# Regrouping the MLP products between the transform slots of a spectral block on TensorE

## Chip, cores and metric

The kernel runs on one core of a Trainium2 chip. The metric is the device time of one execution in microseconds (us). Three runs of the kernel before gave 3795.04, 3796.38 and 3802.16 us, so its median is 3796.38 us.

## What is computed

Four layers follow each other on `x` of shape (4, 64, 128, 128): a box convolution, four spectral blocks (`L1_conv`, which is what the change touches), and two more box convolutions. One spectral block is:

```python
def _block(x, ln1w, ln1b, ln2w, ln2b, w1, w2, b1, b2, mw1, mb1, mw2, mb2):
    residual = x
    xn = _ln(transpose(x, (0, 2, 3, 1)), ln1w, ln1b)
    xf = rfft2(xn, axes=(1, 2), norm='ortho')
    o1 = relu(complex product of xf with w1 + b1)      # 64 x 64 channels
    o2 = complex product of o1 with w2 + b2
    o2 = o2 where |re| > 0.01 or |im| > 0.01, else 0
    x = residual + irfft2(o2)
    h = gelu(_ln(x, ln2w, ln2b) @ mw1 + mb1)           # 64 -> 256
    return x + (h @ mw2 + mb2)                         # 256 -> 64
for i in range(4): x = _block(x, ...)
```

All arithmetic is in float32.

## The kernel before

`afno_layers` works through 16 runs (4 images by 4 layers), one image and layer at a time. All of an image's `x` lies in SBUF. The work is a hand-written software pipeline. A period `n` belongs to run `n` and has 16 steps `q` = 0 to 15, and each step has four slots `s` = 0 to 3. In every step the MLP of run `n` advances by one block of 8 image rows. In the slots the transforms run: the last four inverse products of run `n`, and then forward transform, spectrum, backward transform and first four inverse products of run `n + 1`. Since periods begin at n = -2, the first transform (n = -1) has no MLP beside it, and the last period (n = 15) has no forward transform. Fifteen periods, n = 0 to 14, have both.

Which unit of the transform stands in which slot is set by these lines, where a slot's number is `4 * q + s`:

```python
REST_SLOTS = (3, 7, 17, 18)
FORWARD_SLOT, SPECTRUM_SLOT, BACKWARD_SLOT = 19, 23, 44
NEXT_SLOTS = (48, 49, 51, 53)
```

- `inverse`: a product into two PSUM banks; VectorE (three additions), ScalarE (one copy, `odd`) and GpSimd finish it. Products 4 to 7 of a run stand in slots 3, 7, 17 and 18, so products 6 and 7 are in step 4, slots 1 and 2.
- `forward`: slots 19 to 22, four units of four 128x128 matmuls each (L1629). VectorE and ScalarE take turns copying the result into `g`, four small operations for one unit. The wait before unit 2 is for `s_x` of the last inverse product: `if i == 2 and n: pe.wait_ge(s_x, INVERSES * n)`.
- `spectrum`: slots 23 to 41 hold `t` = 0 to 18. On TensorE each holds three products of three successive chunks: mix2 (L1640, chunk t-2, reads `o1`), mix1 (L1649, chunk t-1, reads `xf`), and fh (L1658, chunk t). ScalarE turns mix1's result into `o1` (L1473) and fh's into `xf` (L1480). VectorE turns mix2's result into `o2` (L1336). Chunk 0 is a quarter as wide as the others. Before fh of chunk 0, TensorE waits for all copies of the forward transform, and for a `memset` of VectorE (L1329) that itself waits for ScalarE's copies.
- `backward`: slots 44 to 47, after GpSimd's masked products of every chunk (L1259).
- `inverse` 0 to 3 of the next run: slots 48, 49, 51, 53.

The MLP of a step is, on TensorE: `mlp_up(Q, 0)` and `mlp_up(Q, 1)` (L1683, 64 rows of the array to a matmul), `mlp_down(Q - 1)` (L1694, 64 columns to a matmul), `turn_back(Q - 2)` (L1709) and `turn(Q + 1)` (L1703), both transposes on the full array. ScalarE does gelu (L1507) after each `mlp_up`, `operand` (L1513) after `turn` and `mlp_delta` (L1520) after `mlp_down`. VectorE's `residual` (L1364) adds the result to `x` after `turn_back`, and the next `mlp_down` waits for it. VectorE's `sum_up` and `root` and ScalarE's `square` (layer-norm statistics), in slots of their own, and ScalarE's `fill_stage` stay where they are.

Each engine walks the periods and steps in its own loop, and its instruction order is the order of that code.

Of the kernel before, what the change touches and what calls it, by code (L numbers as in the profile page):

```python
# [1009 lines left out]
def afno_layers(nc, const, w, src, dst):  # L1010


    with ExitStack() as ctx:
# [118 lines left out]
        with nc.Block() as block:  # L1132
# [146 lines left out]
            def _(dve):  # L1279
# [120 lines left out]
                for n, q in periods():  # L1400
                    Q, r = BLOCKS * n + q, SETS * n + q // 4
                    parts(n, q, 0, inverse, forward, spectrum, backward)
                    if 0 <= Q - 2 < BLOCKS * RUNS:
                        residual(Q - 2)
                    for s in range(1, 4):
                        parts(n, q, s, inverse, forward, spectrum, backward)
                        if s == (3 if q in (5, 12) else 1):
                            for strip in strips_at(n, q):
                                sum_up(*strip)
                        if FIRST_ROOT <= r < END_ROOT:  # L1410
                            if q in (1, 13) and s == 1:
                                root(r, range(ROOT_STEPS))
                            if (q, s) in ((5, 3), (9, 2)):
                                root(r, range(ROOT_STEPS // 2))
                            if (q, s) in ((6, 1), (9, 3)):
                                root(r, range(ROOT_STEPS // 2, ROOT_STEPS))

            @block.scalar
            def _(act):
# [135 lines left out]
                for n, q in periods():  # L1555
# [6 lines left out]
                    parts(n, q, 0, inverse, forward, spectrum, backward)  # L1562
                    if 0 <= Q + 1 < BLOCKS * RUNS:
                        operand(Q + 1)
                    parts(n, q, 0, other, other, magnitude, other)
# [10 lines left out]
                    parts(n, q, 2, inverse, forward, spectrum, backward)  # L1576
                    if 0 <= Q - 1 < BLOCKS * RUNS:
                        mlp_delta(Q - 1)
                    parts(n, q, 2, other, other, magnitude, other)
# [11 lines left out]
            def _(pe):  # L1591
# [120 lines left out]
                for n, q in periods():  # L1712
# [4 lines left out]
                    parts(n, q, 0, inverse, forward, spectrum, backward)  # L1717
                    if 0 <= Q - 2 < BLOCKS * RUNS:
                        turn_back(Q - 2)
                    if 0 <= Q + 1 < BLOCKS * RUNS:  # L1720
                        turn(Q + 1)
                    parts(n, q, 1, inverse, forward, spectrum, backward)
                    if mlp:
                        mlp_up(Q, 1)
                    parts(n, q, 2, inverse, forward, spectrum, backward)
                    if 0 <= Q - 1 < BLOCKS * RUNS:
                        mlp_down(Q - 1)
                    parts(n, q, 3, inverse, forward, spectrum, backward)
# [57 lines left out]
```

## Time and profile before

| | us |
|---|---|
| median of three runs | 3796.38 |
| the profiled execution | 3798.83 |
| its span | 3796.9 |
| TensorE (PE) matmul busy in the span | 3299.8 |
| VectorE (DVE) busy | 2437.3 |
| ScalarE (ACT) busy | 2377.3 |
| GpSimd (POOL) busy | 1713.5 |

In the profile, PE is TensorE's matmuls and PEld its weight loads. A float32 matmul is recorded in passes, so "x8" stands for four matmuls. The end of a matmul is modelled and lies inside the next one, so the cost of a product is read from its start to the start of the next. The spectral blocks take the stretch from about 377 to 3310 us of the span.

### The profile page before, as it was taken

How to read it: one execution, taken by the hardware profiler on the slowest of the kernel's cores; microseconds unless marked ns; L12 is line 12 of the kernel's file. 1: busy time of each engine (PE TensorE's matmuls, PEld its weight loads, DVE VectorE, ACT ScalarE, POOL GpSimd, SP SyncE). 2: the span in 40 equal slices, each digit the busy share in tenths (PEclk: the TensorE clock that was granted, in tenths of full speed). 3: DMA queues.
4: the chain of work that ended last, by engine and by line, in shares of the span. 5: the costliest groups of instructions: out<-in, count | busy, mean ns of one | idle time of the engine just before them, and what ended most of it. 6: DMA issues, size and time to landing. Idle time of an engine off the chain costs nothing. (4 is left out here: it accounts for less than half of the span.)

```text
span 3796.9 us, 54132 instructions
## 1 busy us (share of the span) xinstructions
PE 3299.8 (87%) x18664; PEld 2009.6 (53%) x18664; DVE 2437.3 (64%) x4175; ACT 2377.3 (63%) x3944; POOL 1713.5 (45%) x1397
## 2 busy tenths in 40 slices
PE   2951879999999999898999999999999999777479
PEld 0641746555565646464646464646555565255247
DVE  1843675767676667676766667575757655369567
ACT  0852566667676757676766666666657665547358
POOL 2404445445555554545445454545545533234232
PEclk9985989999999999999999999999999999989779
DMA  9871111111111111213121111111101111263798
GB/s 226 251 249 60 45 50 40 56 39 62 45 45 50 45 45 45 111 45 133 45 84 45 50 40 51 40 50 45 62 29 62 45 45 51 58 263 117 186 261 245
DMA packets 235117, 334.15 MB, mean 88 GB/s; under 512 B 38624, under 2 KB 163680, under 8 KB 228720
## 3 DMA queue, kind: packets, MB, share of 16 engines
q1 hardware_dynamic: 198112, 298.44, 23.2%
q10 hardware_dynamic: 28784, 18.44, 2.1%
q0 software_dynamic: 7968, 13.99, 1.5%
q8 instruction: 147, 2.41, 0.3%
q14 instruction: 106, 0.87, 0.1%
HBM read 183.99 MB, written 146.80 MB: 87 GB/s over the span
## 5 line engine op out<-in xcount | busy, mean ns | idle before, releaser
L1507 ACT ACTIVATE a_hidden<-a_wide,a_up_b 128x1024 f32<-128x1024 f32 x512 | 569.8, 1113 | 136.4 <-PE a_wide L1683 135.0
L1683 PE MATMUL a_wide<-a_yc,a_up_fold 64*128 64x512 f32 x2048 | 583.5, 645 | 52.8 <-ACT a_hidden L1507 48.5
L1694 PE MATMUL a_result<-a_hidden,a_down 128*64 128x512 f32 x2048 | 516.1, 625 | 67.4 <-DVE a_x L1364 66.0
L1259 POOL TENSOR_TENSOR a_y<-a_o,a_mag 128x256 f32<-128x256 f32 (+1 forms) x512 | 365.4, 739 | 385.6 <-DVE a_mag L1353 385.6
L1217 POOL TENSOR_TENSOR a_y<-a_x,a_stat 128x512 f32<-128x512 f32 x256 | 267.9, 1047 | 483.8 <-DVEq L1398 463.6
L1336 DVE TENSOR_TENSOR a_o<-a_bank,a_mix_b 128x512 f32<-128x512 f32 (+1 forms) x272 | 181.6, 668 | 278.4 <-PE a_bank L1640 274.3
L1520 ACT ACTIVATE a_delta<-a_result,a_down_b 128x512 f32<-128x512 f32 x256 | 176.3, 689 | 263.6 <-PE a_result L1694 263.5
L1658 PEld LDWEIGHTS a_bank<-a_dft_h,a_g 128*128 128x128 f32 x2080 | 272.4, 191 | 129.0 <-issue 129.0
L1640 PEld LDWEIGHTS a_bank<-a_mix,a_o 128*128 128x128 f32 x2080 | 252.8, 191 | 150.8 <-issue 132.9
L1205 POOL TENSOR_TENSOR a_x<-a_x,a_odd 128x512 f32<-128x512 f32 (+1 forms) x128 | 161.2, 1259 | 367.9 <-DVE a_x L1306 298.2
L1364 DVE TENSOR_TENSOR a_x<-a_result,a_x 128x512 f32<-128x512 f32 x256 | 176.1, 688 | 225.5 <-PE a_result L1709 223.3
L1694 PEld LDWEIGHTS a_result<-a_hidden,a_down 128*64 128x64 f32 x2048 | 131.3, 139 | 355.5 <-issue 321.3
L1640 PE MATMUL a_bank<-a_mix,a_o 128*128 128x128 f32 x2080 | 298.3, 285 | 5.9 <-DVE a_o L1336 4.1
L1683 PEld LDWEIGHTS a_wide<-a_yc,a_up_fold 64*128 64x128 f32 x2048 | 159.5, 187 | 265.8 <-issue 235.9
L1383 DVE TENSOR_REDUCE a_stat<-a_sq 128x16 f32<-128x1024 f32 x240 | 290.9, 1212 | 11.1 <-ACT a_sq L1541 9.4
L1629 PE MATMUL a_bank<-a_dft_w,a_y 128*128 128x128 f32 x2048 | 245.8, 279 | 57.9 <-POOL a_y L1242 57.6
L1629 PEld LDWEIGHTS a_bank<-a_dft_w,a_y 128*128 128x128 f32 x2048 | 235.6, 193 | 93.1 <-POOL a_y L1242 57.7
L1658 PE MATMUL a_bank<-a_dft_h,a_g 128*128 128x128 f32 x2080 | 277.3, 275 | 1.8 <-DVE a_g L1329 1.8
L1381 DVE TENSOR_REDUCE a_stat<-a_x 128x16 f32<-128x1024 f32 x224 | 271.5, 1212 | 1.9 <-issue 0.2
L1649 PE MATMUL a_bank<-a_xf,a_mix_fold 128*128 128x512 f32 (+1 forms) x544 | 270.0, 578 | 0.8 <-ACT a_xf L1480 0.8
L1673 PEld LDWEIGHTS a_bank<-a_dft_hi,a_y 128*128 128x128 f32 x2048 | 235.7, 193 | 53.7 <-POOL a_y L1259 30.1
L1673 PE MATMUL a_bank<-a_dft_hi,a_y 128*128 128x128 f32 x2048 | 245.8, 279 | 17.5 <-POOL a_y L1259 17.5
(191 smaller groups left out, 6370.1 us busy)
## 6 DMA issues: line engine op xcount, KB each, us to landing
a_x<-rows SPq DMA_DIRECT2D x112, 512.0 KB, 4.5
rows<-a_x SPq DMA_DIRECT2D x112, 512.0 KB, 2.9
box_x<-in_x SPq DMA_DIRECT2D x64, 256.0 KB, 4.3
turned<-box_o SPq DMA_DIRECT2D x64, 256.0 KB, 3.6
a_y<-turned SPq DMA_DIRECT2D x16, 1024.0 KB, 11.0
box_x<-rows SPq DMA_DIRECT2D x16, 1024.0 KB, 24.1
turned<-box_work SPq DMA_DIRECT2D x64, 256.0 KB, 2.0
box_x<-turned SPq DMA_DIRECT2D x64, 256.0 KB, 3.8
```

The lines of the kernel that those rows point to most:

```text
L1217: G.tensor_tensor(rows(y2[:, i % 2]), x[:, row:row + HB], r[:, :, None].broadcast_to([P, HB, C]), ALU.mult).then_inc(s_y2, 1)
L1259: ins = G.tensor_tensor(y[n % 2][:, :, to].rearrange("p c k -> p k c"), o2[:, j % 3, lo:4, r], mask[:, lo:4], ALU.mult)
L1381: V.tensor_reduce(stat[:, 0, r % SETS, kind - 1, u * SH:(u + 1) * SH], strip, AX.X, ALU.add)
L1383: V.tensor_reduce(stat[:, 1, r % SETS, kind - 1, u * SH:(u + 1) * SH], squares_of(r, kind, u), AX.X, ALU.add).then_inc(s_sq_read, 1)
L1507: A(hidden[:, i % 2, j], wide[:], ACT.Gelu, bias=up_b2[:, l, j:j + 1]).then_inc(s_hid, 1)
L1629: mm = M(bank[i % 4][:, c * P:(c + 1) * P], y[n % 2][:, 4 * i + c, :], dft_w[:], start=True, stop=True)
L1640: mm = M(bank[3][:, k * P:(k + 1) * P], o1[:, k * P:(k + 1) * P], mix2[:, l], start=True, stop=True)
L1649: M(bank[2][:, 0:cols], mix1_fold[:, l], xf[:, 0:cols], start=True, stop=True).then_inc(s_mix1, 1)
L1658: mm = M(bank[0][:, k * P:(k + 1) * P], g[:, first_kw(t) + k].rearrange("p r c -> p (r c)"), dft_h[:], start=True, stop=True)
L1673: mm = M(bank[i % 4][:, c * P:(c + 1) * P], y[n % 2][:, 4 * i + c, :], dft_hi[:], start=True, stop=True)
L1683: mm = M(wide[:, half * BANK:(half + 1) * BANK], up_fold[cs, l, j * P:(j + 1) * P], yc[cs, i % 2], start=True, stop=True)
L1694: mm = M(result[half * C:(half + 1) * C, :], down[:, l, j, :], hidden[:, i % 2, j, half * BANK:(half + 1) * BANK], start=j == 0, stop=j == ...
```

## The change

Three of the engines' loops are reordered inside a step. Nothing is added or removed. On TensorE the step was up(0), slot 0, turn_back, turn, slot 1, up(1), slot 2, down, slot 3. It becomes up(0), turn_back, turn, slot 0, slot 1, up(1), down, slot 2, slot 3. ScalarE's and VectorE's steps follow.

```diff
 # VectorE
                 for n, q in periods():
                     Q, r = BLOCKS * n + q, SETS * n + q // 4
-                    parts(n, q, 0, inverse, forward, spectrum, backward)
                     if 0 <= Q - 2 < BLOCKS * RUNS:
                         residual(Q - 2)
+                    parts(n, q, 0, inverse, forward, spectrum, backward)
 # ScalarE
-                    parts(n, q, 0, inverse, forward, spectrum, backward)
                     if 0 <= Q + 1 < BLOCKS * RUNS:
                         operand(Q + 1)
+                    parts(n, q, 0, inverse, forward, spectrum, backward)
                     parts(n, q, 0, other, other, magnitude, other)
...
-                    parts(n, q, 2, inverse, forward, spectrum, backward)
                     if 0 <= Q - 1 < BLOCKS * RUNS:
                         mlp_delta(Q - 1)
+                    parts(n, q, 2, inverse, forward, spectrum, backward)
                     parts(n, q, 2, other, other, magnitude, other)
 # TensorE
                     if mlp:
                         mlp_up(Q, 0)
-                    parts(n, q, 0, inverse, forward, spectrum, backward)
                     if 0 <= Q - 2 < BLOCKS * RUNS:
                         turn_back(Q - 2)
                     if 0 <= Q + 1 < BLOCKS * RUNS:
                         turn(Q + 1)
+                    parts(n, q, 0, inverse, forward, spectrum, backward)
                     parts(n, q, 1, inverse, forward, spectrum, backward)
                     if mlp:
                         mlp_up(Q, 1)
-                    parts(n, q, 2, inverse, forward, spectrum, backward)
                     if 0 <= Q - 1 < BLOCKS * RUNS:
                         mlp_down(Q - 1)
+                    parts(n, q, 2, inverse, forward, spectrum, backward)
                     parts(n, q, 3, inverse, forward, spectrum, backward)
```

TensorE, step 5 of a period, from its second `mlp_up`: the last forward units (L1629), fh of chunk 0 (the first L1658) and what follows. Before:

```order
L1683 MATMUL a_wide<-a_yc,a_up_fold 128x512 x2
L1629 MATMUL a_bank0<-a_dft_w,a_y0 128x128 x4
L1629 MATMUL a_bank1<-a_dft_w,a_y0 128x128 x4
L1629 MATMUL a_bank2<-a_dft_w,a_y0 128x128 x4
L1629 MATMUL a_bank3<-a_dft_w,a_y0 128x128 x4
L1694 MATMUL a_result<-a_hidden,a_down 64x512 x4
L1658 MATMUL a_bank0<-a_dft_h,a_g 128x128
L1683 MATMUL a_wide<-a_yc,a_up_fold 128x512 x2
```

The same place in the changed kernel:

```order
L1683 MATMUL a_wide<-a_yc,a_up_fold 128x512 x2
L1694 MATMUL a_result<-a_hidden,a_down 64x512 x4
L1629 MATMUL a_bank0<-a_dft_w,a_y0 128x128 x4
L1629 MATMUL a_bank1<-a_dft_w,a_y0 128x128 x4
L1629 MATMUL a_bank2<-a_dft_w,a_y0 128x128 x4
L1629 MATMUL a_bank3<-a_dft_w,a_y0 128x128 x4
L1658 MATMUL a_bank0<-a_dft_h,a_g 128x128
L1683 MATMUL a_wide<-a_yc,a_up_fold 128x512 x2
```

`mlp_down` (L1694) stood between the last forward unit and fh of chunk 0. It now stands ahead of the forward units, and fh follows the last of them directly.

TensorE, step 4, from inverse product 6 on (L1611 and L1615 are one inverse product). Before:

```order
L1611 MATMUL a_bank0<-a_g,a_idft_e 128x512
L1615 MATMUL a_bank1<-a_g,a_idft_o 128x512
L1683 MATMUL a_wide<-a_yc,a_up_fold 128x512 x2
L1611 MATMUL a_bank2<-a_g,a_idft_e 128x512
L1615 MATMUL a_bank3<-a_g,a_idft_o 128x512
L1694 MATMUL a_result<-a_hidden,a_down 64x512 x4
L1629 MATMUL a_bank0<-a_dft_w,a_y0 128x128 x4
L1629 MATMUL a_bank1<-a_dft_w,a_y0 128x128 x4
```

The same place in the changed kernel:

```order
L1611 MATMUL a_bank0<-a_g,a_idft_e 128x512
L1615 MATMUL a_bank1<-a_g,a_idft_o 128x512
L1683 MATMUL a_wide<-a_yc,a_up_fold 128x512 x2
L1694 MATMUL a_result<-a_hidden,a_down 64x512 x4
L1611 MATMUL a_bank2<-a_g,a_idft_e 128x512
L1615 MATMUL a_bank3<-a_g,a_idft_o 128x512
L1629 MATMUL a_bank0<-a_dft_w,a_y0 128x128 x4
L1629 MATMUL a_bank1<-a_dft_w,a_y0 128x128 x4
```

`mlp_down` stood between inverse product 7 and the forward transform. It now stands ahead of product 7.

TensorE, step 6, from mix2 of the first chunk (the fourth row is the second `mlp_up`). Changed kernel:

```order
L1640 MATMUL a_bank3<-a_mix2,a_o1 128x128
L1649 MATMUL a_bank2<-a_xf,a_mix1_fold 128x512
L1658 MATMUL a_bank0<-a_dft_h,a_g 128x128 x4
L1683 MATMUL a_wide<-a_yc,a_up_fold 128x512 x2
L1694 MATMUL a_result<-a_hidden,a_down 64x512 x4
L1640 MATMUL a_bank3<-a_mix2,a_o1 128x128 x4
L1649 MATMUL a_bank2<-a_xf,a_mix1_fold 128x512
L1658 MATMUL a_bank0<-a_dft_h,a_g 128x128 x4
L1640 MATMUL a_bank3<-a_mix2,a_o1 128x128 x4
L1649 MATMUL a_bank2<-a_xf,a_mix1_fold 128x512
L1658 MATMUL a_bank0<-a_dft_h,a_g 128x128 x4
```

Before, `mlp_down` stood between the second and the third group of L1640, L1649 and L1658 shown here. Now those two groups touch, and `mlp_up` and `mlp_down` touch.

## Rows read from the trace of the kernel before

**Rows 1.** The page's first part: busy us, share, instructions.

```profile
PE 3299.8 (87%) x18664; PEld 2009.6 (53%) x18664; DVE 2437.3 (64%) x4175; ACT 2377.3 (63%) x3944; POOL 1713.5 (45%) x1397
```

**Rows 2.** Waits of PE, 380:3350: total us, times, longest.

```profile
PE a_result L1694 <- DVE a_x L1364: 66.0, 41, 2.5
```

**Rows 3.** Timeline of PE in a spectrum step: start, us, instructions.

```profile
1506.78 1.06 PE L1640 MATMUL a_bank<-a_mix,a_o 128*128 128x128 f32 x8
1507.68 1.02 PE L1649 MATMUL a_bank<-a_xf,a_mix_fold 128*128 128x512 f32 x2
1508.54 1.05 PE L1658 MATMUL a_bank<-a_dft_h,a_g 128*128 128x128 f32 x8
1509.52 1.13 PE L1683 MATMUL a_wide<-a_yc,a_up_fold 64*128 64x512 f32 x4
1510.58 1.16 PE L1640 MATMUL a_bank<-a_mix,a_o 128*128 128x128 f32 x8
1511.58 1.02 PE L1649 MATMUL a_bank<-a_xf,a_mix_fold 128*128 128x512 f32 x2
...
1513.42 1.94 PE L1694 MATMUL a_result<-a_hidden,a_down 128*64 128x512 f32 x8
1515.29 1.16 PE L1640 MATMUL a_bank<-a_mix,a_o 128*128 128x128 f32 x8
```

**Rows 4.** Timeline of PE, transform without MLP (n = -1), idle in brackets.

```profile
396.80 0.46 PE L1658 MATMUL a_bank<-a_dft_h,a_g 128*128 128x128 f32 x2 [1.84 <-DVE a_g L1329]
...
397.95 1.06 PE L1658 MATMUL a_bank<-a_dft_h,a_g 128*128 128x128 f32 x8
398.85 0.39 PE L1640 MATMUL a_bank<-a_mix,a_o 128*128 128x128 f32 x2
399.70 1.13 PE L1649 MATMUL a_bank<-a_xf,a_mix_fold 128*128 128x512 f32 x2 [0.46 <-ACT a_xf L1480]
...
403.61 1.05 PE L1658 MATMUL a_bank<-a_dft_h,a_g 128*128 128x128 f32 x8
404.55 1.16 PE L1640 MATMUL a_bank<-a_mix,a_o 128*128 128x128 f32 x8
405.55 1.02 PE L1649 MATMUL a_bank<-a_xf,a_mix_fold 128*128 128x512 f32 x2
```

**Rows 5.** Timeline of PE, end of the spectrum to the backward transform.

```profile
1521.98 1.16 PE L1640 MATMUL a_bank<-a_mix,a_o 128*128 128x128 f32 x8
1523.07 1.13 PE L1683 MATMUL a_wide<-a_yc,a_up_fold 64*128 64x512 f32 x4
1524.13 1.94 PE L1694 MATMUL a_result<-a_hidden,a_down 128*64 128x512 f32 x8
1526.00 1.13 PE L1683 MATMUL a_wide<-a_yc,a_up_fold 64*128 64x512 f32 x4
1527.96 3.84 PE L1673 MATMUL a_bank<-a_dft_hi,a_y 128*128 128x128 f32 x32 [0.83 <-POOL a_y L1259]
```

**Rows 6.** Timelines of PE, ACT and DVE at the end of the forward transform.

```profile
1635.51 1.94 PE L1694 MATMUL a_result<-a_hidden,a_down 128*64 128x512 f32 x8
1637.42 0.46 PE L1658 MATMUL a_bank<-a_dft_h,a_g 128*128 128x128 f32 x2
...
1635.62 1.34 ACT L1456 ACTIVATE a_g<-a_bank 64x252 f32<-64x252 f32 x4 [0.45 <-PE a_bank L1629]
...
1637.11 0.17 DVE L1329 MEMSET a_g<- 1x128 f32 x1 [0.83 <-ACT a_g L1456]
```

**Rows 7.** Timelines of PE and DVE at inverse product 6.

```profile
1611.85 1.02 PE L1615 MATMUL a_bank<-a_g,a_idft_o 128*128 128x512 f32 x2
...
1614.33 0.69 DVE L1310 TENSOR_TENSOR a_x<-a_bank,a_x 128x512 f32<-128x512 f32 x1
```

**Rows 8.** Timelines at the next run's inverse product 2, and two steps on.

```profile
1557.37 0.69 DVE L1305 TENSOR_TENSOR a_x<-a_bank,a_x 128x512 f32<-128x512 f32 x1 [2.92 <-PE a_bank L1615]
...
1573.12 3.49 PE L1694 MATMUL a_result<-a_hidden,a_down 128*64 128x512 f32 x8 [2.35 <-DVE a_x L1364]
```

## The prediction, made before the changed kernel was run

> **What bounds the kernel now.** The page's first part puts TensorE at 3299.8 us of matmul in a span of 3796.9 us, with VectorE and ScalarE at about two thirds [rows 1]. The waits of PE over the spectral blocks say how little is left: the largest cause, `mlp_down` waiting for VectorE's `residual`, is 66.0 us in 41 waits [rows 2]. So in these blocks TensorE is the bound, its products run back to back, and a change pays what it saves in TensorE's pitch (start of one product to start of the next) and costs what it uncovers as waits. I then read one spectrum step in PE's timeline for the pitch [rows 3], and as a model of touching slots the one transform that has no MLP beside it, n = -1 [rows 4].
>
> **What it saves.** Full-array products, `mlp_up` (64 rows) and `mlp_down` (64 columns) use the array in three shapes. Four 128x128 matmuls take 0.90 us between full-array neighbours: fh 397.95 to 398.85 [rows 4], mix2 after a transpose 1506.78 to 1507.68 [rows 3]. Before an `mlp_up` fh takes 0.98 us (1508.54 to 1509.52), and mix2 behind it takes 1.00 (1510.58 to 1511.58) [rows 3]. So leaving the full shape costs 0.08 and coming back 0.10. `mlp_up` itself costs 1.06 whether a full-array product follows (1509.52 to 1510.58) [rows 3] or `mlp_down` (1523.07 to 1524.13), and `mlp_down` costs 1.87 before either (1513.42 to 1515.29 [rows 3], 1524.13 to 1526.00 [rows 5]). The change removes a return and a departure only where slot 2 is not empty, because elsewhere up(1) and down touch already. Those are steps 4 to 9 and 11, seven of a period. That is 7 x 0.18 = 1.26 us a period, and over the 15 periods that have both MLP and transforms 19 us. The exit after up(0) stays, in front of `turn_back` instead of slot 0, and I count it as nothing.
>
> The Trainium skill, "TensorEngine Tiling (Array Packing)", section Tiling Modes, says that changing the tiling mode drains TensorE. It gives no price. The rows agree, with 0.08 to 0.10 us for each edge, except that up to down shows none beyond what up always costs.
>
> **What it uncovers.** Four places, each once a period except the third.
>
> First, fh of chunk 0. It waits for the last forward unit's four ScalarE copies and VectorE's `memset` after them. Now `mlp_down` covers this: it starts at 1635.51 when the forward units are through, the copies start at 1635.62, the `memset` at 1637.11, fh at 1637.42 [rows 6]. That is 1.91 us, of which down's 1.87 is work. After the change down stands ahead of the forward units and nothing is left between. Bounds: 1.84, which is what the transform without MLP waits at this very place [rows 4], and 1.91. I take 1.9.
>
> Second, mix1 of chunk 1. It needs `xf`, made from the fh just before it, with only the small mix2 of chunk 0 between. Until now the two transposes lay there too. Without MLP mix1 starts 0.85 us after that mix2 [rows 4], which is one matmul of four, a quarter of 0.90, so 0.22. That leaves 0.63, and 0.10 more because a weight load that follows a wait is not hidden (below). I take 0.73, with the row's idle of 0.46 as the lower bound.
>
> Third, the steady spectrum pairs. In touching slots mix2 follows the mix1 of its own chunk with only one fh between, and ScalarE needs slightly longer for `o1`: fh to mix2 takes 0.94 instead of 0.90, and mix2 1.00 instead of 0.90 [rows 4]. That is 0.14 for each second slot. The pairs are slots 26-27 to 38-39, seven of them, hence 1.0 us a period. Lower bound 0.04 x 7 = 0.3. Pair 24-25 is the second place. In the last pair, 40-41, mix2 follows mix1 of its own chunk with nothing between, and waits about 0.9 for `o1`. But the backward transform waits 0.83 today for GpSimd's end of a chain that starts from this same mix2, 5.98 us before it (1521.98 to 1527.96) [rows 5]. The transposes move from before that mix2 to behind up(0), so they leave one wait and fill the other. Net nothing; if the first wait were covered after all, this would give 0.83 x 15 = 12 us.
>
> Fourth, forward unit 2 waits for `x` of inverse product 7. At product 6 the last addition of VectorE starts at 1614.33 and takes 0.69, so it ends 3.17 us after the second matmul starts at 1611.85 [rows 7]. Until now down (1.87) and two units lay over this. Now it is the rest of the product, 0.86 for a 512-wide matmul [rows 3], and two units of 0.90, together 2.66. That uncovers 0.51, and 0.10 for the weight load: 0.6, between 0.4 and 0.7.
>
> ScalarE's `operand` and `mlp_delta` move ahead of slots 0 and 2. Their inputs (`turn`, `mlp_down`) are now finished when those slots' products start, so no `o1` or `xf` is queued behind a waiting one. VectorE's `residual` is likewise earlier in its queue, and its input too. I cost these at nothing. The cover is the slots' own products ahead of the first result; if it fails, it costs up to one such operation's 0.7 us in a step.
>
> Sum of a period: 1.9 + 0.73 + 1.0 + 0.6 = 4.23 uncovered, less 1.26 saved, is 2.97. Times 15 that is +45 us. The profiled execution took 3798.8 us, so it would take 3844. The median of the runs shown is 2.4 us lower, which gives **3841 us**, 1.2% slower.
>
> **Rivals.**
>
> *The clock falls as well.* After one of its waits TensorE runs a `mlp_down` in 3.49 us, which is the 1.2 GHz level, instead of 1.94 at 2.4 GHz [rows 8, 3]. A new idle of 1.9 us before chunk 0, followed by short work, could bring one more such drop a period: 1.55 x 15 = 23 us, so 3864. Against it: the same idle without MLP is followed by fh at 1.06, full speed [rows 4]. [...] Chance 0.10.
>
> *Faster: the lost time is given back.* TensorE waits for VectorE's backlog in steps 13 and 14, most of the 66.0 us [rows 2]. If that backlog ran on a clock of its own, lateness from earlier in the period would shorten those waits, and only the savings would be left: 3796 - 19 = 3777. It turns into a gain once 2.97 of the 4.23 us a period are recovered. Against it: VectorE's chain there starts after 2.92 us of its own idle, released by TensorE's inverse product [rows 8], so it shifts with TensorE. Chance 0.04.
>
> *No difference.* Only the first place opens, and pairs and inverse product stay covered: 15 x (1.9 - 1.26) = 10 us, and with the last pair's 12 us recovered about nothing, 3794 to 3804. The rows of the transform without MLP speak against it. Chance 0.06.
>
> *Forecast.* Chance 0.80. With all lower bounds (1.84 + 0.46 + 0.3 + 0.4 = 3.0) it is +26 us, 3822; with the upper ones (1.91 + 0.73 + 1.3 with the last pair + 0.7, less 1.26) it is +51, 3847. An end effect or the clock now and then widens this upwards.
>
> **How the numbers follow.** About 0.2%, 8 us, is what a measurement can tell from no change. Slower takes the forecast and the clock, 0.90; same 0.06; faster 0.04. The range for 8 in 10 is 3815 to 3866: it reaches the clock rival above, leaves out the two below.
>
> **What would show it.** Right: PE's waits gain a group at L1658 released by DVE L1329, 15 times some 1.9 us; one at L1649 from ACT, 15 x 0.5; one at L1629 from DVE L1310, 15 x 0.5; and a touching mix2 starts 0.94 after fh. The backward wait (L1673 on GpSimd) shrinks, and one at L1640 from ACT of about 0.9 appears. The waits of steps 13 and 14 stay. Wrong: waits of L1694 that shrink by microseconds a period, or an L1658 that starts at once.

## The result, and the profile of the changed kernel

The changed kernel takes 3858.97 us (median of 4 runs, 3851.67 to 3862.81), the kernel before 3799.2 us in the runs beside it (3795.04 to 3802.16). The ratio is 1.0156, with a 95% interval of 1.0136 to 1.0175. So it is 1.6% slower, 60 us by the medians and 53 us by the profiled executions (3851.67 against 3798.83). The forecast was +45 us. One execution of the kernel of experiment 8 took 9350.06 us, its eleven others 3790 to 3804 us; it is left out of that kernel's ratio.

The first part of the page of the changed kernel, which answers to [rows 1] (busy us, share, instructions):

```profile
PE 3316.7 (86%) x18664; PEld 2016.0 (52%) x18664; DVE 2433.5 (63%) x4175; ACT 2367.9 (62%) x3944; POOL 1708.9 (44%) x1397
```

The same instructions run, and TensorE's busy time has grown by 17 us only. The rest of the 53 is waiting. The waits of PE over 380 to 3400 us (line and releaser, total us, times, longest):

```profile
PE a_result L1694 <- DVE a_x L1364: 67.7, 42, 2.7
...
PE a_bank L1658 <- DVE a_g L1329: 29.3, 16, 1.8
...
PE a_bank L1640 <- ACT a_o L1473: 15.3, 21, 0.9
...
PE a_bank L1673 <- POOL a_y L1259: 8.4, 15, 4.9
...
PE a_bank L1649 <- ACT a_xf L1480: 6.3, 17, 0.5
PE a_bank L1629 <- DVE a_x L1310: 4.9, 15, 0.3
```

Each group that was forecast is there. The first one, `mlp_down` behind VectorE's `residual`, stood at 66.0 [rows 2]: nothing is given back there. One wait of each transform group belongs to n = -1, as in [rows 4].

To place the time I cut each of the 15 periods at four starts on TensorE: the first forward unit (L1629), fh of chunk 0 (L1658), the first backward product (L1673) and the 64-wide inverse product (L1613). One such period in PE's timeline of the changed kernel (start us, us, instruction, idle before it):

```profile
2382.18 1.95 PE L1629 MATMUL a_bank<-a_dft_w,a_y 128*128 128x128 f32 x16
2384.45 0.71 PE L1629 MATMUL a_bank<-a_dft_w,a_y 128*128 128x128 f32 x4 [0.32 <-DVE a_x L1310]
...
2404.26 0.46 PE L1658 MATMUL a_bank<-a_dft_h,a_g 128*128 128x128 f32 x2 [1.83 <-DVE a_g L1329]
...
2478.92 1.27 PE L1673 MATMUL a_bank<-a_dft_hi,a_y 128*128 128x128 f32 x9 [0.24 <-POOL a_y L1259]
...
2499.38 0.33 PE L1613 MATMUL a_bank<-a_g,a_idft_e 128*128 128x64 f32 x2
...
2566.02 1.95 PE L1629 MATMUL a_bank<-a_dft_w,a_y 128*128 128x128 f32 x16
```

The lengths are 22.08, 74.66, 20.46 and 66.64 us. In most periods a stretch repeats within 0.02 us unless the clock falls in it, which adds about 1.6 us, as in the last of these (65.00 without). Three periods in the middle of the execution differ, in the kernel before too. The table gives, for the kernels of this study but those of experiments 6 and 10, the length that a period without a fallen clock has. The transposes of one step lie on the other side of two of the cuts when the first group is moved (about 0.9 us goes from the last stretch to the second), so across kernels the sum is what compares.

| us | forward | spectrum | backward | inverse | period |
|---|---|---|---|---|---|
| before | 19.77 | 72.57 | 20.70 | 65.97 | 179.01 |
| changed | 22.08 | 74.67 | 20.46 | 65.00 | 182.21 |
| first group alone | 19.72 | 74.43 | 20.61 | 65.09 | 179.85 |
| second group alone | 22.12 | 72.87 | 20.50 | 65.87 | 181.36 |
| TensorE's order alone | 22.08 | 74.25 | 20.42 | 65.06 | 181.81 |
| down back in step 5 | 20.20 | 74.68 | 20.46 | 65.00 | 180.34 |
| down back in steps 4, 5 | 19.73 | 74.69 | 20.46 | 65.09 | 179.97 |
| roots a slot earlier | 22.07 | 74.26 | 20.41 | 64.99 | 181.73 |
| all four undone | 19.73 | 73.58 | 20.41 | 65.09 | 178.81 |
| edges only | 19.77 | 72.36 | 20.50 | 65.95 | 178.58 |

A period is 3.20 us longer, where 2.97 were forecast. That is 48 us over 15 periods. The other part is the clock. From fh of chunk 0 to the backward transform five of the 15 periods take 76.27 to 76.31 us instead of 74.67, and none did before: 5 x 1.61 = 8 us. From the first cut to the last the changed kernel takes 61.5 us more (2863.3 against 2801.7). Of the remaining 5 us about 4 lie in two periods, those that start at 1635.98 and 1826.01 us. They are longer in the kernel before too, but the change opens three more waits in each: mix2 waits 0.52 and 0.44 us for ScalarE's `o1`, and a backward product waits 1.06 us for ScalarE. ScalarE's, then PE's timeline there:

```profile
1736.69 2.00 ACT L1552 ACTIVATE a_stage<-a_y 128x1024 f32<-128x1024 f32 x1 [2.90 <-POOL a_y L1229]
...
1739.72 1.49 PE L1673 MATMUL a_bank<-a_dft_hi,a_y 128*128 128x128 f32 x11 [1.06 <-ACT a_g L1499]
```

L1552 is `fill_stage`, 2.00 us long. Of the 15 periods only these two hold it beside the spectrum and the backward transform. That it causes the three waits is read from the rows; no run moves it.

In the profiled execution the parts ahead of the first cut and behind the last gave 4.8 and 3.9 us back, hence 53 there and 60 by the medians.

Here is the clock. PE's timeline behind fh of chunk 0, in a period where it falls, then in one where it does not:

```profile
2218.76 0.46 PE L1658 MATMUL a_bank<-a_dft_h,a_g 128*128 128x128 f32 x2 [1.83 <-DVE a_g L1329]
2219.14 1.60 PE L1683 MATMUL a_wide<-a_yc,a_up_fold 64*128 64x512 f32 x4
2220.68 1.11 PE L1709 MATMUL a_result<-a_ident,a_delta 128*128 128x128 f32 x4
2221.58 1.06 PE L1703 MATMUL a_turned<-a_ident,a_y 128*128 128x128 f32 x4
...
2404.65 1.13 PE L1683 MATMUL a_wide<-a_yc,a_up_fold 64*128 64x512 f32 x4
2405.71 0.66 PE L1709 MATMUL a_result<-a_ident,a_delta 128*128 128x128 f32 x4
2406.20 0.60 PE L1703 MATMUL a_turned<-a_ident,a_y 128*128 128x128 f32 x4
...
2406.86 1.06 PE L1658 MATMUL a_bank<-a_dft_h,a_g 128*128 128x128 f32 x8
2407.76 0.48 PE L1640 MATMUL a_bank<-a_mix,a_o 128*128 128x128 f32 x2
2408.61 1.12 PE L1649 MATMUL a_bank<-a_xf,a_mix_fold 128*128 128x512 f32 x2 [0.37 <-ACT a_xf L1480]
2409.57 1.05 PE L1658 MATMUL a_bank<-a_dft_h,a_g 128*128 128x128 f32 x8
...
2415.34 1.05 PE L1658 MATMUL a_bank<-a_dft_h,a_g 128*128 128x128 f32 x8
2416.28 1.16 PE L1640 MATMUL a_bank<-a_mix,a_o 128*128 128x128 f32 x8
2417.27 1.02 PE L1649 MATMUL a_bank<-a_xf,a_mix_fold 128*128 128x512 f32 x2
```

The windows of the same two places (us, busy us and instructions of PE, PEld, DVE, ACT and POOL, then the granted clock as a share of 2.4 GHz, DMA share, GB/s):

```profile
2220.20:2222.60 2.40, 2.40 (x11) 1.93 (x10) 2.19 (x8) 1.11 (x1) 0.00 (x0) 0.50 0.00 0
2405.70:2408.10 2.40, 2.40 (x22) 2.32 (x20) 2.19 (x8) 2.01 (x4) 0.00 (x0) 1.00 0.00 0
```

Half of 2.4 GHz is granted in the one, the whole of it in the other. The idle ahead of both is the same 1.83 us. The second timeline also shows the second place of the forecast: mix1 of chunk 1 (2408.61) waits 0.37 us for ScalarE's `xf` and starts 0.85 us after mix2 of chunk 0, and 0.96 us pass until the next fh. Ahead of the change these two pitches were 0.22 and 0.86, so this place costs 0.73. The last three rows are a touching pair: mix2 starts 0.94 us after fh, and mix1 0.99 after mix2, the pitches of [rows 4].

A saving that the forecast counted as nothing is in these rows too. Behind `mlp_up` stands now `turn_back`, which takes 0.49 us to the next start (2405.71 to 2406.20). In the kernel before it stood behind a full-array product:

```profile
1505.91 0.60 PE L1709 MATMUL a_result<-a_ident,a_delta 128*128 128x128 f32 x4
1506.35 0.60 PE L1703 MATMUL a_turned<-a_ident,a_y 128*128 128x128 f32 x4
```

There it took 0.44, but the mix2 behind `mlp_up` took 1.00, where behind the transposes it takes 0.90 [rows 3]. So the return to the full array is 0.05 us cheaper in each of the seven steps (5 to 10 and 12) that have a product in slot 0 and no wait that takes it up, about 0.35 us a period.

One number stands where the forecast expected nothing. At the end of the spectrum, PE's and then DVE's timeline:

```profile
2472.51 1.16 PE L1640 MATMUL a_bank<-a_mix,a_o 128*128 128x128 f32 x8 [0.78 <-ACT a_o L1473]
...
2470.39 0.23 DVE L1005 SCALAR_TENSOR_TENSOR a_stat<-a_stat 128x64 f32<-128x64 f32 x1
2470.76 0.69 DVE L1364 TENSOR_TENSOR a_x<-a_result,a_x 128x512 f32<-128x512 f32 x1
2471.37 0.68 DVE L1336 TENSOR_TENSOR a_o<-a_bank,a_mix_b 128x512 f32<-128x512 f32 x1
```

The wait of the last mix2 for `o1` (0.78 us) is the one forecast. But from that mix2 to the backward product 6.41 us pass (2472.51 to 2478.92), where it was 5.98 [rows 5]. VectorE doesn't wait for TensorE here: behind the second half of `root` (it ends with L1005) comes `residual` (L1364), and only then `o2` (L1336), 1.14 us before the mix2 of the chunk after it. The experiments take this place apart.

### The profile page after: what moved, and what is told of

Read it like the earlier page. It is cut to its first block and busy times, and to the rows that moved or that the text cites. A ratio compares the mean times of both kernels' runs of the same rounds, so it can differ in the third digit from the quotient of the medians.

```text
span 3849.8 us, 54132 instructions
## 1 busy us (share of the span) xinstructions
PE 3316.7 (86%) x18664; PEld 2016.0 (52%) x18664; DVE 2433.5 (63%) x4175; ACT 2367.9 (62%) x3944; POOL 1708.9 (44%) x1397
## 5 line engine op out<-in xcount | busy, mean ns | idle before, releaser
L1694 PE MATMUL a_result<-a_hidden,a_down 128*64 128x512 f32 x2048 | 513.9, 623 | 69.1 <-DVE a_x L1364 67.7
L1336 DVE TENSOR_TENSOR a_o<-a_bank,a_mix_b 128x512 f32<-128x512 f32 (+1 forms) x272 | 181.3, 667 | 309.8 <-PE a_bank L1640 308.4
L1364 DVE TENSOR_TENSOR a_x<-a_result,a_x 128x512 f32<-128x512 f32 x256 | 176.4, 689 | 288.3 <-PE a_result L1709 283.9
L1658 PEld LDWEIGHTS a_bank<-a_dft_h,a_g 128*128 128x128 f32 x2080 | 273.3, 192 | 147.2 <-issue 147.2
L1694 PEld LDWEIGHTS a_result<-a_hidden,a_down 128*64 128x64 f32 x2048 | 131.0, 138 | 413.6 <-issue 404.7
L1640 PE MATMUL a_bank<-a_mix,a_o 128*128 128x128 f32 x2080 | 297.9, 285 | 18.6 <-ACT a_o L1473 15.3
L1473 ACT ACTIVATE a_o<-a_bank,a_mix_b 128x512 f32<-128x512 f32 (+2 forms) x272 | 181.2, 666 | 201.2 <-PE a_bank L1649 201.2
L1658 PE MATMUL a_bank<-a_dft_h,a_g 128*128 128x128 f32 x2080 | 277.9, 276 | 29.3 <-DVE a_g L1329 29.3
L1640 PEld LDWEIGHTS a_bank<-a_mix,a_o 128*128 128x128 f32 x2080 | 253.0, 191 | 90.8 <-issue 52.4
L1629 PE MATMUL a_bank<-a_dft_w,a_y 128*128 128x128 f32 x2048 | 243.8, 278 | 62.7 <-POOL a_y L1242 57.6
L1629 PEld LDWEIGHTS a_bank<-a_dft_w,a_y 128*128 128x128 f32 x2048 | 236.4, 193 | 85.2 <-POOL a_y L1242 57.7
L1649 PE MATMUL a_bank<-a_xf,a_mix_fold 128*128 128x512 f32 (+1 forms) x544 | 271.5, 581 | 6.3 <-ACT a_xf L1480 6.3
L1673 PE MATMUL a_bank<-a_dft_hi,a_y 128*128 128x128 f32 x2048 | 239.6, 278 | 10.6 <-POOL a_y L1259 8.4
```

What stands on the lines that cost most here:

```text
L1629: mm = M(bank[i % 4][:, c * P:(c + 1) * P], y[n % 2][:, 4 * i + c, :], dft_w[:], start=True, stop=True)
L1640: mm = M(bank[3][:, k * P:(k + 1) * P], o1[:, k * P:(k + 1) * P], mix2[:, l], start=True, stop=True)
L1649: M(bank[2][:, 0:cols], mix1_fold[:, l], xf[:, 0:cols], start=True, stop=True).then_inc(s_mix1, 1)
L1658: mm = M(bank[0][:, k * P:(k + 1) * P], g[:, first_kw(t) + k].rearrange("p r c -> p (r c)"), dft_h[:], start=True, stop=True)
L1673: mm = M(bank[i % 4][:, c * P:(c + 1) * P], y[n % 2][:, 4 * i + c, :], dft_hi[:], start=True, stop=True)
L1694: mm = M(result[half * C:(half + 1) * C, :], down[:, l, j, :], hidden[:, i % 2, j, half * BANK:(half + 1) * BANK], start=j == 0, stop=j == ...
```

## The experiments

Two theories stood after the result. **Lost cover**: the change opens waits at a few places of TensorE's chain of spectrum products, each of a fixed size, and the two groups add up. The rival: **order on the other engines**, by which moving `operand`, `residual` and `mlp_delta` ahead of slots delays the copies that the slots' products need, and so makes the loss. A third, the **clock**, could hold most of it. Below, diffs against the kernel before are headed so; the others are against the changed kernel. Each kernel was timed 4 to 12 times beside the kernel before; stretches, waits and falls of the clock come from one profiled execution of each. In the text "q" is a step of the period.

### 1. The first group alone

Against the kernel before: of the change, only `turn_back` and `turn` on TensorE, `operand` on ScalarE and `residual` on VectorE move ahead of slot 0.

```diff
                         mlp_up(Q, 0)
-                    parts(n, q, 0, inverse, forward, spectrum, backward)
                     if 0 <= Q - 2 < BLOCKS * RUNS:
                         turn_back(Q - 2)
                     if 0 <= Q + 1 < BLOCKS * RUNS:
                         turn(Q + 1)
+                    parts(n, q, 0, inverse, forward, spectrum, backward)
```

> Only the first group: turn_back and turn stand behind up(0), slots 0 and 1 touch; slot 2 stays between up(1) and down, on all engines. Theory of uncovered waits: nothing is lost ahead of fh of chunk 0 or at forward unit 2 (down still covers both), and no array-shape edge is saved. Uncovered are mix1 of chunk 1 (0.73 us a period), three steady pairs (3 x 0.14) and, as the trace of the changed kernel showed, 0.4 us more in the chain from the last mix2 to the backward transform; the exit after up(0) gives some 0.04 a step back. Together 1.1 to 1.5 us a period, +16 to +23 us against the kernel before. Rival (the loss lies at the fh of chunk 0 alone): within 3 us of before.

3814.78 against 3798.62 us, ratio 1.0046 (1.0029 to 1.0063); a period is 0.84 us longer. Its waits of PE:

```profile
PE a_bank L1640 <- ACT a_o L1473: 15.4, 21, 0.9
...
PE a_bank L1649 <- ACT a_xf L1480: 6.1, 17, 0.4
PE a_bank L1673 <- POOL a_y L1259: 4.9, 1, 4.9
```

So this group holds mix1 of chunk 1 and the last pair. The wait of the backward product is down to the one of n = -1: here the last pair's wait does take its place, as forecast. The extra 0.4 us at the end of the spectrum, which my expectation put into this group, isn't here: the backward transform starts 6.00 us after the last mix2, although `residual` stands ahead of `o2` here too. That is why the period is 0.84 us longer and not 1.1 to 1.5: 0.73, and three steady pairs at 0.15, less 0.35 for the cheaper returns, make 0.83.

### 2. The second group alone

Against the kernel before: only `mlp_down` and `mlp_delta` move ahead of slot 2.

```diff
                         mlp_up(Q, 1)
-                    parts(n, q, 2, inverse, forward, spectrum, backward)
                     if 0 <= Q - 1 < BLOCKS * RUNS:
                         mlp_down(Q - 1)
+                    parts(n, q, 2, inverse, forward, spectrum, backward)
```

> Only the second group: down stands behind up(1), slots 2 and 3 touch; slot 0 stays ahead of turn_back, on all engines. Theory of uncovered waits: 1.9 (fh of chunk 0) + 0.6 (forward unit 2) + 4 pairs x 0.14, less 7 x 0.18 of saved edges = 1.8 us a period, +27 us, and up to +35 with the drops of TensorE's clock that follow the wait at fh of chunk 0. The backward transform's wait on GpSimd stays at about 0.8 us in each of 15 periods. Rival (the pairs of slots are what costs, wherever they lie): about half of the changed kernel's loss, with a pair as dear as one of the first group's.

3833.72 against 3798.62 us, ratio 1.0096 (1.0081 to 1.0112); a period is 2.35 us longer. Together the two groups make 0.84 + 2.35 = 3.19 us a period, and the whole change 3.20. They add up, and the second holds the larger part. Its waits of PE:

```profile
PE a_bank L1673 <- POOL a_y L1259: 24.4, 16, 4.9
```

The waits at fh of chunk 0 and at forward unit 2 are as in the changed kernel. The backward product's wait, which I expected to stay at 0.8 us, is longer than the 0.83 of [rows 5]: (24.4 - 4.9) / 15 = 1.30 us. DVE's, then PE's timeline at the end of the spectrum:

```profile
2459.47 0.23 DVE L1005 SCALAR_TENSOR_TENSOR a_stat<-a_stat 128x64 f32<-128x64 f32 x1
2459.91 0.69 DVE L1336 TENSOR_TENSOR a_o<-a_bank,a_mix_b 128x512 f32<-128x512 f32 x1 [0.21 <-DVE a_stat L1005]
...
2460.75 1.16 PE L1640 MATMUL a_bank<-a_mix,a_o 128*128 128x128 f32 x8
...
2467.19 1.05 PE L1673 MATMUL a_bank<-a_dft_hi,a_y 128*128 128x128 f32 x7 [1.30 <-POOL a_y L1259]
```

From the last mix2 to the backward product 6.44 us pass, so the late `o2` is in this group. `residual` doesn't stand ahead of it here; `root` alone does. What makes `root` late is that slots 2 and 3 of step 9, behind which its halves stand, now touch; in experiment 9 they touch as well, with `root` a slot earlier, and the backward transform is not late. With that the sum of my theory closes: its 1.8 and this 0.46 us make 2.3, against 2.35 measured.

### 3. TensorE's order alone

TensorE as in the changed kernel, ScalarE's and VectorE's calls where they stood before (`mlp_delta` moves back likewise).

```diff
+                    parts(n, q, 0, inverse, forward, spectrum, backward)
                     if 0 <= Q - 2 < BLOCKS * RUNS:
                         residual(Q - 2)
-                    parts(n, q, 0, inverse, forward, spectrum, backward)
...
+                    parts(n, q, 0, inverse, forward, spectrum, backward)
                     if 0 <= Q + 1 < BLOCKS * RUNS:
                         operand(Q + 1)
-                    parts(n, q, 0, inverse, forward, spectrum, backward)
```

> TensorE in the order of the changed kernel, ScalarE and VectorE in the order of before (operand behind slot 0, mlp_delta behind slot 2, residual behind slot 0). Theory: those moves are worth nothing in themselves, so the time is that of the changed kernel within 5 us, with the same waits at fh of chunk 0, mix1 of chunk 1 and forward unit 2. Rival (operand and delta ahead of the slots delay o1 and xf): 10 us or more faster than the changed kernel, with a touching mix2 that starts 0.90 instead of 0.94 us after fh.

3843.91 against 3798.62 us, ratio 1.0121 (1.0101 to 1.0142); a period of 181.81 us. So TensorE's order alone makes 2.80 of the 3.20 us, and the rival falls for the bulk. The time is 13 us below the changed kernel by the ratios, where I expected at most 5; the two intervals overlap slightly. The other 0.40 is real, and lies in the spectrum stretch alone (74.25 against 74.67). DVE's, then PE's timeline at the end of the spectrum:

```profile
2288.37 0.69 DVE L1336 TENSOR_TENSOR a_o<-a_bank,a_mix_b 128x512 f32<-128x512 f32 x1 [0.28 <-PE a_bank L1640]
...
2289.64 0.68 DVE L1364 TENSOR_TENSOR a_x<-a_result,a_x 128x512 f32<-128x512 f32 x1
...
2289.97 1.16 PE L1640 MATMUL a_bank<-a_mix,a_o 128*128 128x128 f32 x8 [0.78 <-ACT a_o L1473]
...
2295.97 1.23 PE L1673 MATMUL a_bank<-a_dft_hi,a_y 128*128 128x128 f32 x9
```

With `residual` behind `o2`, VectorE waits for TensorE (0.28) instead of being late, `o2` starts 1.60 us ahead of the mix2 instead of 1.14, and the backward product starts 6.00 us behind it with no wait. The last pair's 0.78 is unchanged. This run puts three calls back at once, so that it is the place of `residual` is read from these rows. TensorE's touching mix2 products keep their pitch of 0.94 and 1.00 us, so those don't come from ScalarE's or VectorE's order.

### 4. `mlp_down` back behind slot 2 in step 5

```diff
-                    if 0 <= Q - 1 < BLOCKS * RUNS:
+                    if 0 <= Q - 1 < BLOCKS * RUNS and not q == 5:
                         mlp_down(Q - 1)
                     parts(n, q, 2, inverse, forward, spectrum, backward)
+                    if 0 <= Q - 1 < BLOCKS * RUNS and q == 5:
+                        mlp_down(Q - 1)
```

`mlp_delta` on ScalarE is treated alike.

> The changed kernel, but in step 5 of every period mlp_down (TensorE) and mlp_delta (ScalarE) stand behind slot 2 again, between the last forward units and fh of chunk 0. Theory of uncovered waits: fh of chunk 0 waits 0.0 instead of 1.8 us, one return edge and one departure edge come back (0.18), so 1.7 us a period and 26 us less than the changed kernel, and the slow-clock stretches right behind fh of chunk 0 go as well (another 8 us): 26 to 34 us faster than the changed kernel, +25 to +33 against before. Rival (that wait only shifts to the next one): under 10 us faster than the changed kernel.

3817.03 against 3798.62 us, ratio 1.005 (1.0037 to 1.0064). The forward stretch falls from 22.08 to 20.20 us: fh of chunk 0 costs 1.88. The waits of PE for `memset` are gone apart from the one of n = -1, and the clock falls behind fh of chunk 0 in none of the 15 periods. So one product, left where it was, gives back 40 us of the 60 by the ratios (1.0156 to 1.005). My expectation was 26 to 34; the stretches and the falls of the clock account for 28 + 8 = 36. The 1.88 is net: the departure edge of `mlp_down` in step 5, 0.10 us, has come back with it, so the wait itself costs about 1.98.

### 5. The roots a slot earlier

The halves of VectorE's `root` in step 9 stand behind slots 1 and 2 instead of 2 and 3, so that the second is through before the last pair.

```diff
-                            if (q, s) in ((5, 3), (9, 2)):
+                            if (q, s) in ((5, 3), (9, 1)):
                                 root(r, range(ROOT_STEPS // 2))
-                            if (q, s) in ((6, 1), (9, 3)):
+                            if (q, s) in ((6, 1), (9, 2)):
                                 root(r, range(ROOT_STEPS // 2, ROOT_STEPS))
```

> The changed kernel with VectorE's two halves of root in step 9 one slot earlier (behind slots 1 and 2 instead of 2 and 3). In the changed kernel those halves stand behind two slots that now touch, VectorE comes late to the next o2, and the backward transform starts 6.4 us after the last mix2 instead of 6.0. Theory: that 0.4 us is VectorE's root, so it goes: backward starts 6.0 us after the last mix2 and the wait on GpSimd is 0, 6 us less than the changed kernel. Rival (it is ScalarE's mlp_delta or the place of residual): no difference, the distance stays at 6.4.

3840.13 against 3796.85 us, ratio 1.0125 (1.011 to 1.0139). The spectrum stretch is 74.26 us, and the backward product's wait is that of n = -1 alone:

```profile
PE a_bank L1673 <- POOL a_y L1259: 4.6, 1, 4.6
```

This is the same 0.41 us as in experiment 3, with `residual` left ahead of slot 0. In TensorE's changed order either of the two, `root` or `residual`, taken from in front of `o2` is enough: the queue of both is what is late. In the order of experiment 2 `root` alone was. By the ratios this kernel is 12 us faster than the changed one, where I expected 6. The 0.41 us make 6, and the clock falls behind fh of chunk 0 in three periods instead of five, which makes another 3.

### 6. The gap filled

Ahead of fh of chunk 0 TensorE runs eight more 128x128 matmuls of the identity into the `turned` bank. Nobody reads them, and they compute nothing of the reference.

```diff
                         if t == 0:
+                            if n:
+                                pe.wait_ge(s_yc, BLOCKS * (n - 1) + 5 + 2)
+                                for c in range(8):
+                                    M(turned[:, c % 4 * P:(c % 4 + 1) * P], ident[:], ident[:], start=True, stop=True)
                             pe.wait_ge(s_g_dve, GROUPS // 2 * (n + 1))
```

> The changed kernel with eight extra 128x128 matmuls on the identity matrix, written to the free bank of the transposes, in front of TensorE's wait at fh of chunk 0 (1.8 us of work that nobody reads). Theory: the wait itself stays, now as work; what goes are the stretches at the 1.2 GHz level that follow it in some periods (fh of chunk 0 to the backward transform takes 76.3 us there instead of 74.7). So all periods take 74.7 or less, and the whole is 0 to 8 us faster than the changed kernel, never slower by more than 2. Rival (the drops are not due to that idle): as many stretches of 76.3 as before.

3846.98 against 3796.85 us, ratio 1.013 (1.0115 to 1.0144). PE's timeline, in which L1655 is the added line:

```profile
2220.68 1.95 PE L1655 MATMUL a_turned<-a_ident 128*128 128x128 f32 x16
2222.67 0.46 PE L1662 MATMUL a_bank<-a_dft_h,a_g 128*128 128x128 f32 x2
2223.06 1.13 PE L1687 MATMUL a_wide<-a_yc,a_up_fold 64*128 64x512 f32 x4
```

The work fills the idle and fh starts no later. The forward stretch is 22.08 us as in the changed kernel, in all but two periods (22.21 and 22.37), so the 1.88 us are not a matter of the clock. The clock falls behind it in 0 of 15 periods instead of 5, which is what these falls cost: 8 us. The same count in the other profiles: 5 of 15 in experiment 2, 7 in experiment 3 and 3 in experiment 5, which all have the idle, and none in experiments 1, 4 and 7 to 10 and in the kernel before, where `mlp_down` covers it. By the ratios it is 10 us faster than the changed kernel, but the intervals (1.0115 to 1.0144, 1.0136 to 1.0175) overlap.

### 7. `mlp_down` back in steps 4 and 5

As experiment 4, with `q in (4, 5)` in place of `q == 5`.

> The kernel of e4 with mlp_down and mlp_delta behind slot 2 in step 4 as well, so that down again lies between inverse product 7 and the forward transform. Theory: forward unit 2 no longer waits for x (0.6 us a period at most; the trace of e4 puts the stage from the first forward unit to fh of chunk 0 0.43 us above before), and step 4 loses its two saved edges (0.18). So that stage returns to 19.8 us, and the kernel is 4 to 6 us faster than e4, +13 to +17 against before. Rival: the wait moves to the next forward unit and the stage stays at 20.2.

3815.61 against 3797.18 us, ratio 1.0052 (1.0039 to 1.0065), no different from experiment 4 by the medians, where I expected 4 to 6 us less. The stretches resolve what the median does not: the forward one falls by another 0.47 us (19.73), and 0.09 comes back in the inverse one, where an edge of array shapes returns. So forward unit 2 costs 0.38 us a period net, 6 us in all. The return edge of `mlp_down`, 0.10 us, lies inside the forward stretch and has come back as well, so the wait itself costs 0.57.

### 8. All four places undone

The kernel of experiment 7 with the roots a slot earlier, and in step 6 slot 0 back ahead of `turn_back` and `turn`, `operand` and `residual`. On TensorE, against experiment 7:

```diff
+                    if q == 6:
+                        parts(n, q, 0, inverse, forward, spectrum, backward)
                     if 0 <= Q - 2 < BLOCKS * RUNS:
                         turn_back(Q - 2)
                     if 0 <= Q + 1 < BLOCKS * RUNS:
                         turn(Q + 1)
-                    parts(n, q, 0, inverse, forward, spectrum, backward)
+                    if not q == 6:
+                        parts(n, q, 0, inverse, forward, spectrum, backward)
```

> The kernel of e9, with root in step 9 a slot earlier and, in step 6 only, slot 0 ahead of turn_back and turn again, so that mix1 of chunk 1 is covered. What is left of the change is grouping in steps 6 to 9 and 11 and touching slots 0 and 1 in steps 7 to 9. Theory: the account is complete, so undoing its four items takes a no-drop period from 3.2 us above before to between 0.3 below and 0.1 above, and the kernel is within 5 us of before. Rival (something else in the change costs, not in the account): 8 us or more above before, although none of the four waits is there.

3798.51 against 3797.18 us, ratio 1.0003 (0.9994 to 1.0012). The period falls from 179.97 to 178.81, by 1.16 us. Of these 0.41 are the roots (experiment 5), so mix1 of chunk 1 is worth about 0.75. The changed order of all other steps is now no loss, a period 0.20 us shorter than before, although the last pair still waits for `o1`:

```profile
PE a_bank L1648 <- ACT a_o L1476: 16.2, 22, 0.9
```

(L1648 and L1476 are L1640 and L1473 moved by the added lines.)

### 9. Edges only

Against the kernel before: `mlp_down` and `mlp_delta` ahead of slot 2 in steps 6, 7, 8, 9 and 11 alone, where the spectrum and the backward transform have room, and the roots a slot earlier as in experiment 5. The first group is not touched.

```diff
+                    if 0 <= Q - 1 < BLOCKS * RUNS and (q in (6, 7, 8, 9, 11)):
+                        mlp_down(Q - 1)
                     parts(n, q, 2, inverse, forward, spectrum, backward)
-                    if 0 <= Q - 1 < BLOCKS * RUNS:
+                    if 0 <= Q - 1 < BLOCKS * RUNS and not (q in (6, 7, 8, 9, 11)):
                         mlp_down(Q - 1)
```

> The kernel before, with down (and mlp_delta) behind up(1) only in steps 6 to 9 and 11, and root's halves in step 9 one slot earlier. So no wait at fh of chunk 0 or forward unit 2 is uncovered and the transposes stay where they were. Theory: steps 6 to 9 save 0.18 of edges each and pay 0.14 for the pair of slots that touches, step 11 saves 0.18: 0.35 us a period, 5 us, 0.1% faster than before, at the limit of what can be measured; the stage from fh of chunk 0 to backward takes 72.4 us against 72.57. Rival (a touching pair costs more than the edges give back): slower than before by 5 us or more.

3788.64 against 3796.85 us, ratio 0.9981 (0.9973 to 0.999): 8 us below the kernel before. It is the only kernel here whose interval lies below 1. A period is 0.43 us shorter, 0.20 of it in the backward stretch, which is the edge pair of step 11, forecast at 0.18, and 0.21 in the spectrum, where four edge pairs (0.72) are set against four touching pairs (0.56). The backward transform starts 5.95 us after the last mix2. What the earlier roots alone do to the kernel before was not run.

### 10. Swapped products

An attempt to take the 0.14 us from a touching pair: experiment 9, with mix1 ahead of mix2 at t = 3, 7, 11 and 15, and `o1` in two buffers in turn (the second is the space of `odd`).

```diff
-        o1 = sb("o1", [P, BANK])
+        o1_own = sb("o1", [P, BANK])
+        o1 = (o1_own[:], odd[:].rearrange("p h c -> p (h c)"))
...
+                    for product in ((mix1_product, mix2_product) if t in (3, 7, 11, 15) else (mix2_product, mix1_product)):
+                        product()
```

> The kernel of e7 with the pair's cost attacked too: in the first of the two touching slots mix1 goes ahead of mix2, and o1 has two buffers (the second is odd, which is free then), so ScalarE makes o1 one product earlier and the second slot's mix2 finds it ready. Theory: fh to the touching mix2 takes 0.90 and mix2 0.90, the pair costs 0 to 0.05 instead of 0.14 (xf is then what comes just in time), so 0.7 to 0.9 us a period in all, 10 to 14 us, 0.3% to 0.4% faster than before. Rival (xf is as late as o1 was): no better than e7.

3798.78 against 3796.85 us, ratio 1.0004 (0.9994 to 1.0015), and its period of 178.98 us is 0.40 longer than that of experiment 9. PE's and DVE's timeline (L1669 is fh, L1646 mix2, L1657 mix1):

```profile
2374.87 1.13 PE L1657 MATMUL a_bank<-a_xf,a_mix_fold 128*128 128x512 f32 x2
2375.84 1.05 PE L1646 MATMUL a_bank<-a_mix,a_odd 128*128 128x128 f32 x8
2376.73 1.06 PE L1669 MATMUL a_bank<-a_dft_h,a_g 128*128 128x128 f32 x8
2377.76 1.13 PE L1646 MATMUL a_bank<-a_mix,a_o 128*128 128x128 f32 x8
...
2376.93 0.69 DVE L1337 TENSOR_TENSOR a_o<-a_bank,a_mix_b 128x512 f32<-128x512 f32 x1 [2.42 <-PE a_bank L1646]
```

My expectation of 10 to 14 us below the kernel before failed. From fh to the mix2 of the next pair 1.03 us pass, more than the 0.94 that the swap was to remove. `o1` has room now, but the earlier mix2 stands later, and the next one needs its bank free: VectorE reads it until 2376.93 + 0.69 = 2377.62, 0.14 us before the mix2 starts. That reading fits the rows; no run with a second bank separates it.

## Why the prediction was right, and where it was not

Direction and size were right: a loss on TensorE's chain, +45 forecast, +53 and +60 measured, inside 3815 to 3866. By its own steps, in us a period, with the edges counted apart from the waits as the forecast did:

| step | forecast | measured | by |
|---|---|---|---|
| fh of chunk 0 | 1.9 | 1.98 (1.88 net) | experiment 4 |
| mix1 of chunk 1 | 0.73 | 0.73 to 0.75 | timeline, experiment 8 |
| forward unit 2 | 0.6 | 0.57 (0.38 net) | experiment 7 |
| seven touching pairs | 1.0 | 7 x (0.04 or 0.05 + 0.10) = 1.0 | timeline |
| edges saved | -1.26 | about -1.2, of it 0.20 in step 11 | timeline, experiment 9 |
| returns behind up(0) | 0 | -0.35 | timeline, experiment 1 |
| last pair and backward | 0 | 0.41 to 0.46 | experiments 2, 3, 5 |
| the period | 2.97 | 3.20 | |

The measured rows add up to 3.1 to 3.2.

- **fh of chunk 0** had bounds of 1.84 and 1.91, and the transform without MLP was a true model of it [rows 4]. The forecast left out here the 0.10 us for the weight load behind a wait, which it counted at mix1 and at forward unit 2. The same model gave the pitches of touching slots.
- **Forward unit 2** came out as worked out. Its idle is 0.32 us, and the rest is the late start and the weight load around it.
- **Edges** cost what the rows said wherever one could be seen alone. One half of one pair saves nothing: in step 5 `mlp_down` returned to the full array at fh of chunk 0, whose one matmul takes 0.39 us to the next start in both kernels.
- **A term put at nothing that is worth something** is "I count it as nothing", for the exit behind up(0). It gives 0.35 us a period back.
- **The step that failed** is "Net nothing" for the last pair, and with it "I cost these at nothing" for VectorE. TensorE's part of it was right: the 0.78 us wait appeared and the old one went (experiment 1). What it overlooked is that VectorE's second half of `root` stands in the same queue. With slots 2 and 3 of step 9 touching, `root` is late to the `o2` behind it, and the backward transform starts 6.4 us after the last mix2 instead of 6.0. The place of `residual` decides only on top of that: with the first group alone `residual` stands ahead of `o2` and nothing is late (experiment 1), and with the second group alone it does not and `o2` is late (experiment 2).
- **Luck.** The two terms that were put at nothing have opposite signs and nearly the same size, so the sum of a period is closer than its parts. The rest of the distance between +45 and +60 is mostly the clock (8 us) and the two periods with `fill_stage` (4 us), and neither is in the sum.
- **The clock** was a rival with a chance of 0.10, priced at 1.55 us in every period. It came true in part: 1.61 us in five of 15. The forecast's argument against it, that n = -1 shows the same idle with full speed behind it, was one instance of an outcome that goes both ways. The runs agree that the idle is a condition (no fall in any kernel where it is covered or filled, 20 in the 60 periods of the four kernels that have it), but it is not enough by itself. The Trainium skill, "TensorE: Matmul & The Clock Gate", section HAM oscillation, describes a kernel in which the clock falls back in every wait for data between two bursts of matmuls. Its waits are longer than this one of 1.83 us, and here not every wait does it.
- **Given back later** did not happen: the waits for `residual` stand at 67.7 us against 66.0.
- Left open: which periods the clock falls in, about 1 us outside the regular period, and the 9 us that the parts ahead of the first cut and behind the last gave back in the profiled execution.

## What to carry to other kernels

A product that belongs to something else, put between two products of a dependent chain, is a cover, and grouping like shapes takes it away: weigh the 0.18 us of an edge against what the chain's other engines need at each place apart, and group only where they have room. Moving `mlp_down` in five steps, with the roots a slot earlier, gained 8 us; the whole regrouping lost 60. When slots are drawn together, look through the queue of each engine that serves them for rare work that used to fit in between: here VectorE's `root`, which stands in a few steps of a period, and ScalarE's `fill_stage`, in two periods of 15. And run each group alone: what made `o2` late in the whole change could have been `root` or `residual`, and experiments 1 and 2 tell which group brought it.

## What was not expected of the hardware

The same 1.83 us of idle on TensorE was followed by 1.2 GHz for about 3 us in five periods and by 2.4 GHz in ten, with the same instructions on both sides. Eight idle-filling matmuls with no reader kept 2.4 GHz in all 15. Even so they did not gain more than the measurement can tell (10 us, with overlapping intervals, against 8 that the five falls cost).
